# A Mamba-style block with an FP6 side branch: another order of the last step on four engines

## What is computed

```python
xn = layernorm(x)
# attn branch (state space block)
xz = xn @ W_in.T;  x_inner, z = split(xz)            # 512 + 512 channels
x_conv = silu(causal_conv4(x_inner) + conv_b)
s_C = (x_conv @ W_x.T)[..., 16:]                     # 16 states
h[t] = 0.95 * h[t-1] + x_conv[t]
y = h * (s_C @ exp(B_log).T) * silu(z)
y = y @ W_out.T
attn = layernorm(xn + y) * ln_g + ln_b
# ffn branch: blocks of 32 features scaled to FP6 range, rounded, scaled back
out = x + attn + dequantised(xn) @ dequantised(weight).T + bias
```

## Time and profile before

| | us |
|---|---|
| median of 3 runs | 264.28 |
| lowest, highest | 263.95, 264.28 |
| the profiled execution | 264.83 |
| its span, first to last instruction | 263.0 |
| VectorE busy | 228.6 (87%) |
| TensorE busy | 216.9 (82%) |
| GpSimd busy | 200.9 (76%) |
| ScalarE busy | 154.6 (59%) |

### The profile page before, as it was taken

How to read it: one execution, slowest core, us unless ns; L and a number is a source line. 1 busy time by engine, 2 the same in 40 slices (tenths; PEclk the granted TensorE clock), 3 DMA queues, 4 the chain that set the end, 5 groups by cost and what they waited for, 6 DMA issues and landing times.

```text
span 263.0 us, 3473 instructions
## 1 busy us (share of the span) xinstructions
PE 216.9 (82%) x1252; PEld 180.8 (69%) x1252; DVE 228.6 (87%) x311; ACT 154.6 (59%) x234; POOL 200.9 (76%) x130
## 2 busy tenths in 40 slices
PE   0369974878899999879999969879999992977991
PEld 0348843357689886668898928767988951867991
DVE  3899999997799899958999999588999997594875
ACT  2796591455956537667995347728976364454320
POOL 1427949999997779999689599979498999933423
PEclk9999999797999999999999999979999998697999
DMA  7965000000000000004112000000202000002032
GB/s 230 262 217 159 1 2 0 0 1 0 0 2 0 1 2 0 0 2 150 40 53 80 0 0 1 2 0 0 82 0 80 4 0 0 0 2 80 26 137 80
DMA packets 10809, 11.18 MB, mean 42 GB/s; under 512 B 680, under 2 KB 10152, under 8 KB 10792
## 3 DMA queue, kind: packets, MB, share of 16 engines
q1 hardware_dynamic: 9520, 9.96, 11.8%
q10 hardware_dynamic: 1272, 0.99, 1.4%
HBM read 6.76 MB, written 4.19 MB: 42 GB/s over the span
## 4 chain that ended last, share of the span: by engine, by line
DVE 33%; POOL 27%; PE 16%; issue 10%; ACT 10%; DMA 4%; POOLq 0%; ACTq 0%; DVEq 0%
POOL hy L420 9%; POOL rstd L400 6%; DVE hy L1139 6%; POOL xc L412 6%; DVE xc L1110 6%; DVE fx L1177 3%; DVE rs L1167 2%; DMA y<-fx 2%; ACT xn L625 2%; DVE fx L1169 2%; DVE bn L1047 2%; DVE y_lo L1157 2%; DVE xq L1093 2%; ACT rs L718 2%; ACT y_hi L694 2%
## 5 line engine op out<-in xcount | busy, mean ns | idle before, releaser
L807 PE MATMUL slot<-xn_hi,w_in_lo 128*128 128x512 f32 x128 | 53.2, 416 | 6.1 <-DVE xn_lo L1099 2.6
L412 POOL TENSOR_TENSOR xc<-xc,tap 128x1021 f32<-128x1021 f32 x16 | 46.1, 2883 | 13.9 <-DVE xc L1110 13.9
L808 PE MATMUL slot<-xn_lo,w_in_hi 128*128 128x512 f32 x128 | 51.6, 403 | 0.0
L809 PE MATMUL slot<-xn_hi,w_in_hi 128*128 128x512 f32 x128 | 51.4, 402 | 0.0
L1139 DVE TENSOR_TENSOR_SCAN hy<-decay,xc 128x1024 f32<-128x1024 f32 x16 | 46.5, 2909 | 0.1
L420 POOL TENSOR_TENSOR hy<-hy,sz 128x1024 f32<-128x1024 f32 x14 | 43.4, 3098 | 2.3 <-ACT sz L672 2.3
L1110 DVE SCALAR_TENSOR_TENSOR xc<-slot,cw,xc 128x1023 f32<-128x1023 f32 (+1 forms) x32 | 40.2, 1265 | 2.1 <-ACT tap L662 1.6
L807 PEld LDWEIGHTS slot<-xn_hi,w_in_lo 128*128 128x128 f32 x128 | 24.7, 193 | 17.6 <-issue 3.9
L677 ACT ACTIVATE xc<-xc 128x1024 f32<-128x1024 f32 x16 | 17.0, 1060 | 29.0 <-POOL xc L412 29.0
L809 PEld LDWEIGHTS slot<-xn_hi,w_in_hi 128*128 128x128 f32 x128 | 24.7, 193 | 6.1
L808 PEld LDWEIGHTS slot<-xn_lo,w_in_hi 128*128 128x128 f32 x128 | 24.8, 193 | 4.9
(11 more groups left out here) (125 smaller groups left out, 586.3 us busy)
## 6 DMA issues: line engine op xcount, KB each, us to landing
x_in<-L_attn_x SPq DMA_DIRECT2D x3, 1024.0 KB, 5.4
y<-fx SPq DMA_DIRECT2D x6, 512.0 KB, 3.0
x_in<-L_attn_x SPq DMA_DIRECT2D x2, 512.0 KB, 4.1
rs<-L_attn_W_in SPq DMA_DIRECT2D x2, 512.0 KB, 10.0
y<-x_in SPq DMA_DIRECT2D x3, 256.0 KB, 2.1
fx<-L_attn_W_out SPq DMA_DIRECT2D x1, 512.0 KB, 12.9
fx<-L_ffn_weight ACTq DMA_DIRECT2D x1, 256.0 KB, 5.3
xc<-L_attn_B_log ACTq DMA_DIRECT2D x1, 256.0 KB
```

The lines of the kernel that those rows point to most:

```text
L412: pool.tensor_tensor(xc[:, c, TAPS - 1:], xc[:, c, TAPS - 1:], tap0[:, c % 2, 0:n], ALU.add).then_inc(conv_ready, 1)
L807: pe.matmul(dst, w_lo, m_hi, start=first, stop=False)
L808: pe.matmul(dst, w_hi, m_lo, start=False, stop=False)
L809: return pe.matmul(dst, w_hi, m_hi, start=False, stop=last)
```

## The change

The same calls are made in another order, from the end of the step before the last on. No instruction is added or removed, and no helper is changed.

```diff
 POOL last_step
                 gate(here, 1)
                 gate(here, 2)
+                gate(here, 3)
+                dequantise(here, 0)
                 rstd_2(prev, 0)
-                dequantise(here, 0)
-                gate(here, 3)
-                scale_g(prev, 0)
                 for c in LAST_YLO_POOL:
                     y_low(here, c)
                 dequantise(here, 1)
+                scale_g(prev, 0)
                 rstd_2(prev, 1)
                 scale_g(prev, 1)
 ACT last_step
                 silu_z(here, 2)
+                s_high(here)
                 squares(prev, 0)
-                s_high(here)
                 silu_z(here, 3)
-                norm_2(prev, 0)
                 y_high(here, 0)
                 y_high(here, 1)
                 y_high(here, 2)
+                y_high(here, 3)
+                norm_2(prev, 0)
                 xd_high(here, 0)
-                y_high(here, 3)
                 squares(prev, 1)
+                xd_high(here, 1)
                 norm_2(prev, 1)
-                xd_high(here, 1)
 PE step
                 z_half(nxt, 2)
+                slot_free(nxt, (tap1_done, NCH * nxt + 3, nxt))
+                s_product(nxt)
                 if is_last(nxt):
                     out_tile(here, 5)
-                slot_free(nxt, (tap1_done, NCH * nxt + 3, nxt))
-                s_product(nxt)
                 slot_free(nxt, (tap1_done, NCH * nxt + 4, nxt))
                 z_half(nxt, 3)
 PE last_step
                 cb_product(here, 3)
+                out_tile(prev, 7)
                 pe.wait_ge(y_ready, NCH * here + 3)
                 t_deq(here, 0)
-                out_tile(prev, 7)
                 last_y_part(0)
 DVE last_step
                 scan(here, 3)
+                s_low(here)
+                take_tile(prev, 5)
                 quantise(here, 0)
-                quantise(here, 1)
-                take_tile(prev, 5)
-                s_low(here)
                 y_product(here, 0)
                 y_product(here, 1)
+                quantise(here, 1)
                 y_product(here, 2)
                 take_tile(prev, 6)
                 y_low(here, 1)
                 y_product(here, 3)
                 y_low(here, 2)
+                take_tile(prev, 7)
                 y_low(here, 3)
                 xd_low(here, 0)
-                take_tile(prev, 7)
-                finish(prev, 0)
                 take_last(0)
                 take_last(1)
                 xd_low(here, 1)
+                finish(prev, 0)
                 take_last(2)
-                finish(prev, 1)
                 finish_group(0)
                 take_last(3)
                 take_last(4)
                 finish_group(1)
+                finish(prev, 1)
                 take_last(5)
```

## The result

The changed kernel takes 260.34 us in the median of 4 runs (259.93 to 261.53), against 264.18 before; the ratio of the paired runs is 0.9849 with a 95% interval of 0.9815 to 0.9883. The forecast was 260.1, the range 258.8 to 263.0. The profiled execution took 259.93, with a span of 258.0. Run once more beside other kernels, the changed kernel gave 260.62 (260.3 to 262.13), ratio 0.988 (0.9809 to 0.9952). Every ratio here compares executions in the fast state only: one run of the kernel with the earlier rstd and one of the kernel before beside it were slow, at 259.12 and 266.58 us.

What follows compares the result with a forecast made beforehand. Bound by TensorE's waits for `s_low` (5.6 us) and tile 7's take (3.1), with half clock behind, VectorE and GpSimd taking turns. Tiles 6.1 us earlier, low clock and small losses leave -4.2: 264.28 - 4.2 = 260.1 us, range 258.8 to 263.0.

Steps and rivals of the forecast that it cites:

- State product: On TensorE, product ahead of old tile 5: inserts 1.0 us idle, buys nothing, on the path once `s_low` comes early.
- the sum: Whole span of 263.0: -5.1 at full clock, -4.2 with low clock behind the gap; median 259.2 or 260.1.
- `s_low` first: On VectorE: `cb_product` 0 at 217.5 instead of 222.21, 12 matmuls in 2.8 instead of 5.25 us, `out_tile` 6 at 220.3.
- VectorE: VectorE's order in the last step: tile 7 taken until 228.6 instead of 238.04; wait of 3.1 us shrinks to some 0.5.
- GpSimd: GpSimd's chain in the last step: dequantisation 0 until 224.3, `scale_g(prev, 0)` 235.4, `scale_g(prev, 1)` 241.6, first group's `rstd` 242.6.
- 2.9 us given as a sign: On GpSimd, listed under what would show the forecast: first dequantisation takes 2.9 us (the other turn: 1.9).
- TensorE until the second transposes: TensorE behind tile 6: second transposes end at 234.9 instead of 244.0, 9.1 us earlier.
- The new gap: TensorE ahead of tile 5: idles 3.3 us for a bank, `take_last(3)` standing behind `finish_group(0)`; tile 5 from 244.9.
- The half clock behind it: TensorE's tiles 5 and 6 likely run partly at lower clock: bounds 0 and 1.5 us, 0.9 showing.
- `finish(prev, 1)`: On VectorE between group 1 and tile 5, 1.2 us: 0.8 us late for tile 7 at full clock, hidden with low clock.
- The rival of the other turn: Dequantisation 0 goes before quantisation 1; first group's `rstd` 3.9 us later, time 261.6 to 263.1; chance 0.22.
- the tail: Stretch from the start of chunk 3's scan on VectorE (212.12 before) to the end; forecast span 258.8 with low clock.

Runs made afterwards that it cites:

- the earlier rstd: Takes-first order (takes of last batch's tiles 3, 4, 5 earlier) plus `rstd_2(prev, 1)` ahead of `scale_g(prev, 0)` on GpSimd: 256.13 us, ratio to before 0.9706.
- the product back: Changed kernel with the state product behind old tile 5 again on TensorE: 260.51 us, ratio 0.9858.
- the takes first: Changed kernel with takes of last batch's tiles 3 and 4 before `finish_group(0)`, tile 5's before `finish_group(1)` and `finish(prev, 1)`: 256.39 us, ratio to before 0.9691.
- the shorter gate: Changed kernel with the last batch's gate of chunk 3 leaving out the last 128 tokens: 263.61 us, ratio to before 0.9962.

## Why the prediction was right

Times after are given as they stand; add 0.6 for the prediction's clock.

1. *State product, 1.0 us "on the path".* Wrong in that word, without harm to the sum. The gap was 0.97 us, but with the product back the time is the same. The end hangs on GpSimd's chain, and that one starts at the end of gate 2: the first quantisation and then gate 3 follow it, whether silu z 3 comes 1.0 us sooner or not. The sum did go by that chain, so the 1.0 us was never in it.
2. *`s_low` first.* `cb_product` 0 at 216.88 (217.5), its 12 matmuls in 2.8 us (2.8), tile 6 at 219.68 (220.3).
3. *VectorE.* Old tile 7's take starts at 227.11 and ends at 227.9 (228.6).
4. *GpSimd.* The dequantisation until 223.84 (224.3), `scale_g(prev, 0)` until 234.9 (235.4), `scale_g(prev, 1)` until 241.1 (241.6), the first group's rstd until 242.1 (242.6). The waits in between fell on other calls than said, with nearly the same sum: 0.85 us were booked at `rstd` and 1.1 at `y_low` 0, and they came at `ve` (1.20 us instead of 0.23) and `nmr` (1.03 instead of 0.20). Nor did the first dequantisation take the 2.9 us given as a sign: it took 1.91, and its dummy in front took the wait (1.22).
5. *TensorE until the second transposes.* They start at 233.61 and end at 234.4 (234.9).
6. *The new gap.* 3.1 us measured (3.3), tile 5 at 244.48 (244.9). That VectorE's order of group and take makes it, the run with the takes first shows.
7. *The half clock behind it.* It came. Tile 5 takes 2.72 us from its first matmul (244.48) to its first ffn matmul (247.20), where tile 3 takes 1.43 (236.73 to 238.16), and 0.1 more in the next seven: 1.4 us, near the upper of the bounds of 0 and 1.5; how much of it shows at the end, 0.9 in the sum, no run separates. The clock in two stretches, the gap and behind it:

```profile
241.00:244.00 3.00, 0.39 (x4) 1.00 0.00 0
244.00:247.00 3.00, 2.52 (x12) 0.51 0.00 0
```

8. *`finish(prev, 1)`* (247.37) is hidden, as said for a half clock. The span ends 2.2 us behind VectorE's last instruction (255.83), as before, so no store was held up.

The rival of the other turn was priced at 261.6 to 263.1 for the run shown, that is 1.5 to 3 us over the forecast; made to happen, it cost 3.0. The way was as said, with the first group's rstd 3.7 us later behind the scan (3.9 said); the clock went another way, with half clock in tile 0's first part and none behind the gap. The tie was near: the prediction has the quantisation 0.06 us ahead of the dequantisation, and measured it is 0.04 us ahead of the dummy. In each profiled execution with these two calls in this order (the changed kernel twice, the product back, the takes first with and without the earlier rstd) it was ahead, by 0.04 to 0.06 us, so the turn repeats; that it fell the way of the forecast was luck all the same, since no row of before could tell it.

The stage came out closer than the whole: forecast for the tail 258.8 - 212.12 = 46.7 us, measured 46.5 twice. That the median lies 0.2 us from the forecast is in part luck. The interval of the ratio is 0.9 us to either side, more than the 0.5 us that the prediction took for the resolution.

## What to carry to other kernels

When work on an in-order engine waits for a factor that comes late, put the calls that free buffers for the bottleneck engine ahead of it: here two lines moved were worth 3.6 us of tail, where the whole reordering before them gave 4.4. They give it only with the other engines' new orders; with the old ones they give nothing. Move in each engine's order first what the engine with the gap waits for, and then look at what is late next, since the gain of one move is often waited for again at the next place (5.7 us at tile 7 instead of 3.1). And when two engines exclude each other on SBUF, who asks first matters: a gate shorter by 0.35 us cost 3 us.

## What had not been expected of the hardware

**The part ahead of the change varies by up to 3.4 us.** The scan of chunk 3 starts between 210.3 and 213.7 us in the profiled executions, with the same code up to about 207 us in all of them. One of the steps can be seen: from the scan of batch 2's chunk 3 to that of batch 3's chunk 0 it is 30.4 us in the execution with the shorter gate (162.63 to 193.05), and 31.7 in the one with the product back (163.87 to 195.57). In both TensorE has the same two waits there, of 0.9 and 1.85 us, until 173.48 and 174.70. Behind them the second has a stretch of half clock, the first has none (stretch, busy, granted clock, the second kernel first):

```profile
175.00:180.00 5.00, 5.00 (x26) 0.66 0.00 0
```

```profile
175.00:180.00 5.00, 5.00 (x30) 1.00 0.00 0
```

Which gaps of TensorE are followed by half clock thus differs between executions. I take this for the source of the spread among the runs of before (262.32 to 266.54 in 19 runs of one chip); that it is the only one is not shown. For a question on one stage the length of that stage in the trace is therefore the better measure: the changed kernel's two profiled executions agree in the tail to 0.1 us, and in the span to 0.8. Of the other kernels one execution each was profiled.

**A dummy of one element waits like a whole tile.** GpSimd's `held_pool` of one element took 1.22 us beside a quantisation, 0.19 without. With it in front, the dequantisation did not get ahead of the quantisation either. The reverse was not seen with a small operation: in the trace of before the `rstd` of 128x4 that stands at 50.34 to 52.35 on GpSimd did not hold up a quantisation that started at 51.52 and took 1.21 us.
